# Attention on one core: nine slots per pair of sequences instead of ten, with the token transposes of the next pair inside the last projection

## The chip, the core and the metric

One core of a Trainium2 chip runs the whole program. The metric is the device time of one execution in microseconds (us), the median over runs. TensorE (PE) does matmuls and transposes, VectorE (DVE) and ScalarE (ACT) work from PSUM and SBUF, GpSimd (POOL) works from SBUF alone, and SyncE (SP) issues all the transfers.

## What is computed

```python
h = s4d_kernel(...)                       # 16 sequences x 128 channels x 1024
h = concatenate([h, txt], axis=1)         # 16 x 205 tokens x 1024
# attention, 32 heads of 32, ONE shared key and value head, causal, ALiBi
qkv = layernorm(h) @ Wqkv                 # 1024 x (1024 + 32 + 32)
p = softmax(causal(q k^T * 32**-0.5 + slope * (pos_k - pos_q)))
h = h + (p v) @ Wo
# feed forward: base linear, and a routed rank-16 LoRA of 8 experts
h = h + ffn(layernorm(h))
```

All of it is float32. Products that need full precision are made of three matmuls: each operand is split into a rounded `hi` part and the rest `lo`, and hi*hi, hi*lo and lo*hi are summed in one PSUM bank.

## The kernel before, in words

Three blocks follow one another: the mixer (the S4D kernel, into `h_dram`), attention, and the block with the output projection and the feed forward. The change lies in `attention_block` alone.

Attention goes by **pairs** of sequences: 8 pairs (`PAIRS`) of 410 tokens (`PT`). `visit` (L504) runs `body` once for pair 0, then a hardware loop (`Fori`) over pairs 1 to 6, once for pair 7, and once more (pair 8, `last is None`) to drain. So the loop branches back five times.

A pair has 10 **slots** (`SLOTS`), a slot has 8 **groups** (`GH`). In each group every engine does its piece of up to four strands. PE's order in a group is: the scores of one head, the three transposes of one head's probabilities (`turn`), a piece of the slot's main work, and in group 6 `values`.

- **Main work** (`MAIN`, L473): slot 0 is `"ln"`, the transposes of the normalised tokens `ht` into `xT` (one token tile and one half of the model dimension in each of the 8 groups); the other nine slots are projections (`("q", k)` or `"kv"`) of 8 x 3 matmuls of 410 columns each (`three`, L642).
- **Attention units**: a pair has 8 units j of 8 heads each. `SCORE_SLOT` gives the slot in which unit j's scores are made: 5, 6, 7, 8, 9, and 11, 12, 13, which are slots 1, 2 and 3 of the next pair. The probabilities of a unit are transposed in groups 4 to 7 of the slot behind (`tj`) and in groups 0 to 3 of the second slot behind (`aj`), where `values` also stands. So slots 0 and 4 have no scores.
- **The split of a main result**: ACT copies the bank rounded (`hi_part`), DVE subtracts (`lo_part`) and so frees the bank. All main work goes round three PSUM banks (`BANKS`), with one count of uses for the pair (`BANK_USES` 18, `USE`, `KV_USE`, `VT_USE`; semaphores `proj_done`, `hi_written`, `bank_read`).
- **DVE** in a group: `bias_head` (adds the mask to the scores and takes the minimum), then a `lo_part` if one is due, then at times a step of the next pair's layer norm (`ln_stats` from turn 12 on, then `ln_rstd`, `ln_apply` from turn 36 on; a turn is 8 * slot + group), then `copy_turned`, which copies the transposed probabilities out of PSUM.
- **SP** stacks q for the scores: `stack_q` (L545) issues three transfers from `q_hi` and `q_lo` into `Qs` in the slot after q was made. The scores of units 2g and 2g + 1 wait for the stacks of q 2g and 2g + 1 (`q_stacked`). SP also loads the next pair's tokens `ht`, in slot 1.

The lines that set PE's waits around the change:

```python
def three(out, w, cols, i):                                   # a projection, group i
def main_step(p, slot, what, i):
    if what == "ln":                                          # slot 0
        wait_count(pe, bank_read, BANK_USES * p + i - BANKS + 1)
def bias_head(p, j, i):                                       # DVE, waits for scores_done
def lo_part(p, slot, i):                                      # DVE, waits for hi_written
```

Of the kernel before, what the change touches and what calls it, by code (L numbers as in the profile page):

```python
# [24 lines left out]
S = CH + TXT  # L25
# [16 lines left out]
SLOTS = 10  # L42
BANKS = 3
BANK_USES = 18
# [372 lines left out]
def attention_block(nc, ctx, io, W):  # L417
# [41 lines left out]
    proj_done, hi_written, bank_read = sem("proj_done"), sem("hi_written"), sem("bank_read")  # L459
# [13 lines left out]
    MAIN = ["ln", ("q", 0), ("q", 1), "kv", ("q", 2), ("q", 3), ("q", 4), ("q", 5), ("q", 6), ("q", 7)]  # L473
    USE = {0: 8, 1: 9, 2: 11, 3: 12, 4: 14, 5: 15, 6: 16, 7: 17}
    KV_USE, VT_USE = 10, 13
    V_SLOT = 6
    LN_HI_AFTER, LN_LO_AFTER = 1, 2
    SCORE_SLOT = [5, 6, 7, 8, 9, 11, 12, 13]

    def hi_count(use):  # L480
        return use + 1 if use < VT_USE else use
# [47 lines left out]
    with nc.Block() as block:  # L529
        @block.sync  # L530
        def _(sp):
# [6 lines left out]
            def stack_q(p, k):  # L538
                g, r = k // 2, k % 2

                wait_apart(sp, bank_read, BANK_USES * p + USE[k] + 1, const_loaded, 32)
# [16 lines left out]
            def body(p, first, last):  # L558
                for slot, main, sj, tj, aj in slots(p, first, last):
                    if last is None and slot == 1:  # L560
# [12 lines left out]
                    if slot == 1 and last is True:  # L573
                        for k in range(4):
                            sp.wait_ge(proj_done, BANK_USES * p + 4 + k + 1)
                            load_wo(k)
# [21 lines left out]
        def _(pe):  # L598
            def scores(p, j, i):
                g, b = j // 2, j % 2  # L600
                if i == 0:
                    for q in q_stacked:
                        pe.wait_ge(q, 16 * STACKS * (4 * p + g + 1))
                    if j == 0:
                        pe.wait_ge(bank_read, BANK_USES * p + KV_USE + 1)
# [19 lines left out]
            def values(p, j):  # L625
# [3 lines left out]
                if j == 0:  # L629
                    pe.wait_ge(bank_read, BANK_USES * p + VT_USE + 1)  # L630
# [14 lines left out]

            def main_step(p, slot, what, i):
                if what == "ln":
                    wait_count(pe, bank_read, BANK_USES * p + i - BANKS + 1)
                    s, half = i % 4, i // 4
                    if half == 0:  # L650
                        pe.wait_ge(xn_ready, 4 * p + s + 1)
                    n = TILES[s][2]
                    for q in range(4):
                        last = nc.tensor.transpose(pr[i % BANKS][:, 128 * q:128 * q + n],
                                                   ht[0:n, s, (4 * half + q) * 128:(4 * half + q + 1) * 128], ident[0:n, 0:n])
                    last.then_inc(proj_done, 1)
                    return
                use = KV_USE if what == "kv" else USE[what[1]]
                if i == 0:
                    if slot == V_SLOT:  # L660

                        wait_apart(pe, bank_read, BANK_USES * p + VT_USE - BANKS + 1, const_ready)
                        for c in range(2):
                            nc.tensor.transpose(pr[VT_USE % BANKS][:, 64 * c:64 * c + HD], vT[96:128, c * S:c * S + CH], ident[96:128, 96:128])
                            last = nc.tensor.transpose(pr[VT_USE % BANKS][0:TXT, 64 * c + HD:64 * c + 2 * HD],
                                                       vT[96:128, c * S + CH:(c + 1) * S], ident[96:128, 96:128])
                        last.then_inc(proj_done, 1)
# [636 lines left out]
```

## Time and profile before

| what | before |
|---|---|
| median of 3 runs | 1744.44 us |
| the runs | 1738.39, 1744.44, 1744.45 us |
| span of the profiled execution, first to last instruction | 1737.4 us |
| PE busy over the span | 1523.9 us, 88% |
| DVE, ACT, POOL busy | 1132.7, 739.4, 537.0 us |
| ACT's split of four token transposes (`xT_hi`, L712), mean | 514 ns |
| mean granted TensorE clock | 0.946 of full |
| attention's projections, first to last | 222.57 to 950.97 us |

The profiled execution is told by its span alone; no time of its own stands beside it. The median lies 7.0 us above that span. In the views of the trace a matmul's busy time overlaps the next one's, since matmuls are pipelined; what a matmul costs PE is the distance from its start to the start of the next. "[2.15 <-X]" behind a row is the idle time of that engine just before it, and what ended it; "issue" is time in which nothing that the profile shows was waited for. A row of the windows view gives the stretch (us from the span's start), its length, then busy time and number of instructions of PE, PEld (weight loads), DVE, ACT and POOL, the mean granted clock, the busy share of the DMA engines and GB/s.

### The profile page before, as it was taken

How to read it: one execution, taken by the hardware profiler on the slowest of the kernel's cores; microseconds unless marked ns; L12 is line 12 of the kernel's file. 1: busy time of each engine (PE TensorE's matmuls, PEld its weight loads, DVE VectorE, ACT ScalarE, POOL GpSimd, SP SyncE). 2: the span in 40 equal slices, each digit the busy share in tenths (PEclk: the TensorE clock that was granted, in tenths of full speed). 3: DMA queues.
4: the chain of work that ended last, by engine and by line, in shares of the span. 5: the costliest groups of instructions: out<-in, count | busy, mean ns of one | idle time of the engine just before them, and what ended most of it. 6: DMA issues, size and time to landing. Idle time of an engine off the chain costs nothing. (4 is left out here: it accounts for less than half of the span.)

```text
span 1737.4 us, 31406 instructions
## 1 busy us (share of the span) xinstructions
PE 1523.9 (88%) x9622; PEld 1296.2 (75%) x9622; DVE 1132.7 (65%) x4116; ACT 739.4 (43%) x2624; POOL 537.0 (31%) x314
## 2 busy tenths in 40 slices
PE   0355399989999999999998769999999999999998
PEld 0355388878878788888887558888888888888886
DVE  7999378879787877879878854344443444444343
ACT  3455157776877767767878631101001010010100
POOL 1787314443534343444545401010110101011010
PEclk9876689999999999999999689999999999999999
DMA  6134455444554445444555341212112121121201
GB/s 200 37 88 94 103 98 109 80 78 91 87 103 73 103 73 103 78 79 97 87 118 86 102 174 37 73 42 67 61 47 72 36 72 48 60 72 36 73 34 38
DMA packets 110527, 139.63 MB, mean 80 GB/s; under 512 B 13156, under 2 KB 96484, under 8 KB 110040
## 3 DMA queue, kind: packets, MB, share of 16 engines
q1 hardware_dynamic: 110408, 138.41, 34.8%
q14 instruction: 89, 0.73, 0.2%
q8 instruction: 30, 0.49, 0.1%
HBM read 62.82 MB, written 40.30 MB: 59 GB/s over the span
## 5 line engine op out<-in xcount | busy, mean ns | idle before, releaser
L700 ACT ACTIVATE P<-P,nmax 128x128 f32<-128x128 f32 (+1 forms) x1024 | 434.3, 426 | 90.3 <-DVE nmax L790 84.0
L764 POOL TENSOR_TENSOR P<-P,rden 128x512 f32<-128x512 f32 (+1 forms) x256 | 329.2, 1308 | 449.2 <-DVE rden L796 449.0
L790 DVE CUSTOM_DVE_ANT_0 P<-sc,mask 128x128 f32<-128x128 f32 (+1 forms) x1024 | 292.3, 323 | 98.4 <-PE sc L612 91.9
L1116 POOL TENSOR_TENSOR h<-h,base_b 128x1024 f32<-128x1024 f32 (+1 forms) x26 | 84.7, 3260 | 637.5 <-DVE xn L1143 637.5
L802 DVE COPY PTR<-pt 128x282 f32<-128x282 f32 x512 | 222.3, 435 | 32.1 <-PE pt L622 18.7
L642 PE MATMUL pr<-xT_hi,wq_hi 128*128 128x410 f32 x576 | 242.4, 421 | 0.0
L642 PE MATMUL pr<-xT_lo,wq_hi 128*128 128x410 f32 x576 | 203.6, 353 | 0.0
L642 PE MATMUL pr<-xT_hi,wq_lo 128*128 128x410 f32 x576 | 202.6, 352 | 0.0
L700 ACT ACTIVATION_READ_ACCUMULATOR P<-P,nmax 128x1 f32 (+1 forms) x1024 | 191.8, 187 | 0.0
L1086 ACT ACTIVATE x2T_hi<-x 128x512 fp32r<-128x512 f32 (+1 forms) x52 | 28.0, 590 | 366.8 <-PE x L1050 366.8
L1028 PE MATMUL wo<-wq_hi,aT_hi 128*128 128x512 f32 (+1 forms) x416 | 168.9, 406 | 12.4 <-DVE aT_lo L1147 7.5
L620 PE MATMUL pt<-ident,P 128*128 128x128 f32 x512 | 152.1, 297 | 27.4 <-DVE PTR L802 26.9
L411 PE MATMUL mix_ps<-Q,X 128*128 128x128 f32 x512 | 75.0, 320 | 112.9 <-DVE Q L393 112.9
L1028 PE MATMUL wo<-wq_lo,aT_hi 128*128 128x512 f32 (+1 forms) x416 | 166.7, 401 | 0.0
L1028 PE MATMUL wo<-wq_hi,aT_lo 128*128 128x512 f32 (+1 forms) x416 | 166.0, 399 | 0.0
L1028 PE MATMUL b<-w_lo,x2T_hi 128*128 128x512 f32 (+1 forms) x416 | 165.8, 398 | 0.0
L1028 PE MATMUL b<-w_hi,x2T_hi 128*128 128x512 f32 (+1 forms) x416 | 164.0, 394 | 0.0
L1028 PE MATMUL b<-w_hi,x2T_lo 128*128 128x512 f32 (+1 forms) x416 | 163.4, 393 | 0.0
L411 PEld LDWEIGHTS mix_ps<-Q,X 128*128 128x128 f32 x512 | 73.7, 235 | 114.0 <-issue 114.0
L611 PE MATMUL sc<-Ks,Qs 100*128 100x128 f32 x512 | 130.6, 255 | 20.5 <-DMA Qs<-q_lo 13.1
L612 PE MATMUL sc<-Ks,Qs 100*77 100x206 f32 x512 | 140.9, 275 | 0.0
L611 PEld LDWEIGHTS sc<-Ks,Qs 100*128 100x128 f32 x512 | 99.8, 195 | 47.6 <-issue 32.0
(180 smaller groups left out, 3185.9 us busy)
## 6 DMA issues: line engine op xcount, KB each, us to landing
Qs<-q_hi SPq DMA_DIRECT2D x128, 205.0 KB, 4.7
Qs<-q_lo SPq DMA_DIRECT2D x64, 205.0 KB, 5.5
att_dram<-att SPq DMA_DIRECT2D x64, 205.0 KB, 2.4
at<-att_dram SPq DMA_DIRECT2D x25, 512.0 KB, 4.7
h<-h_dram SPq DMA_DIRECT2D x25, 512.0 KB, 3.4
out<-h SPq DMA_DIRECT2D x25, 512.0 KB, 2.6
h_dram<-Y SPq DMA_DIRECT2D x64, 128.0 KB, 3.1
ht<-h_dram SPq DMA_DIRECT2D x16, 512.0 KB, 5.1
```

The costliest lines, as they stand in the source:

```text
L411: last = nc.tensor.matmul(out, x[:, step % 2, j].rearrange("p a c -> p (a c)"), Q[:, step % QRING, j, :], start=first, stop=not first)
L611: nc.tensor.matmul(bank[:, 0:CH], q[:, 0:CH], Ks[0:QR, g // 2, b, 0:CH], start=True, stop=True)
L612: nc.tensor.matmul(bank[0:TXT, CH:CH + S + 1], q[:, CH:S], Ks[0:QR, g // 2, b, :], start=True, stop=True).then_inc(scores_done, 1)
L620: nc.tensor.transpose(bank[:, 0:CH], src[:, 0:CH], ident[:])
L642: last = nc.tensor.matmul(out, w[a][:, i, cols], xT[x][:, i, :], start=(i == 0 and m == 0), stop=(i == KC - 1 and m == 2))
L700: last = nc.scalar.activation(P[rows, j % 2, i, cols], P[rows, j % 2, i, cols], ACT.Exp, scale=-1.0, bias=nmax[at], accum_out=den[at])
L764: lastp = nc.gpsimd.tensor_tensor(w, w, r, ALU.mult)
L790: lastv = v.tensor_tensor_reduce(P[0:n, j % 2, i, cols], sc[i % 2][0:n, cols], mask[0:n, m], 1.0, 3.0e38, ALU.add, ALU.min, nmax[0:n, j % ...
L802: v.tensor_copy(PTR[:, j % 2, i, :], pt[i % 2][:, 0:S + TXT]).then_inc(pT_copied, 1)
L1028: last = nc.tensor.matmul(bank[0:n, 0:cols.stop - cols.start], lhs[a][:, k, 0:n], w[b][:, k, cols], start=(start and k == 0 and m == 0), s ...
L1086: nc.scalar.activation(xT[0][:, 4 * half:4 * half + 4, 0:n], src, ACT.Copy).then_inc(xT_hi, 1)
L1116: nc.gpsimd.tensor_tensor(h2[0:n, par, :], h2[0:n, par, :], base_b[0:n, :], ALU.add).then_inc(biased, 1)
```

## The change

- The slot `"ln"` goes; a pair has nine slots, in the order q0, q1, q2, kv, q3, ..., q7. q2 now stands ahead of kv.
- `SCORE_SLOT` becomes 5 to 12: units 0 to 3 in slots 5 to 8, units 4 to 7 in slots 0 to 3 of the next pair. Only slot 4 has no scores.
- The token transposes are grouped by chunk of the model dimension: `turn_ln(p, i)` makes chunk i for all four token tiles (four transposes into one bank). The next pair's stand in slot 8, behind the q7 matmuls of group i. They use banks 0 and 1 in turn; q7 has bank 2.
- ACT splits chunk i one group later (`hi_ln`), DVE two groups later and behind `bias_head` (`lo_ln`); chunks 6 and 7 fall into groups 0 and 1 of the next slot 0, for ACT chunk 7 alone. There q0's first group waits for the split of chunk 6.
- Pair 0's transposes are made ahead of the first slot, and the first waits until all four tiles are normalised.
- SP loads the next pair's tokens at the start of slot 0 instead of slot 1, ahead of the stack of q7.
- The bank counts are split into `main_*`, `ln_*` and `vt_*`.

```diff
-SLOTS = 10
+SLOTS = 9
...
-    MAIN = ["ln", ("q", 0), ("q", 1), "kv", ("q", 2), ("q", 3), ("q", 4), ("q", 5), ("q", 6), ("q", 7)]
+    MAIN = [("q", 0), ("q", 1), ("q", 2), "kv", ("q", 3), ("q", 4), ("q", 5), ("q", 6), ("q", 7)]
...
+    MAIN_BANK = [0, 1, 0, 1, 0, 1, 0, 1, 2]
+    VT_BANK = 2
     V_SLOT = 6
+    LN_SLOT = SLOTS - 1
     LN_HI_AFTER, LN_LO_AFTER = 1, 2
-    SCORE_SLOT = [5, 6, 7, 8, 9, 11, 12, 13]
+    SCORE_SLOT = [5, 6, 7, 8, 9, 10, 11, 12]
...
+                    if slot == 0 and last is False:
+                        sp.wait_ge(ln_turned, KC * p + KC)
+                        for s in range(4):
+                            load_h(p + 1, s)
...
-                    if slot == 1 and last is False:
-                        for s in range(4):
-                            sp.wait_ge(proj_done, BANK_USES * p + 4 + s + 1)
-                            load_h(p + 1, s)
...
+            def turn_ln(p, i):
+
+                if i == 0:
+                    pe.wait_ge(xn_ready, 4 * p + 4)
+                    wait_count(pe, main_read, SLOTS * p - 2)
+                elif i == 1:
+                    wait_count(pe, main_read, SLOTS * p - 1)
+                else:
+                    pe.wait_ge(ln_read, KC * p + i - 1)
+                for s, (c, t0, n) in enumerate(TILES):
+                    at = c * S + t0
+                    last = nc.tensor.transpose(pr[i % 2][:, at:at + n], ht[0:n, s, i * 128:(i + 1) * 128], ident[0:n, 0:n])
+                last.then_inc(ln_turned, 1)
...
+                    if slot == 0:
+                        pe.wait_ge(ln_read, KC * p + KC - 1)
+                    elif slot == 1:
+                        pe.wait_ge(ln_read, KC * p + KC)
+                    elif slot == SLOTS - 1:
+                        pe.wait_ge(vt_read, p + 1)
+                    else:
+                        pe.wait_ge(main_read, SLOTS * p + slot - 1)
+                if i == KC - 1 and slot == 0:
+                    pe.wait_ge(ln_read, KC * p + KC)
...
                         if main is not None:
                             main_step(p, slot, main, i)
+                        if slot == LN_SLOT and last is False:
+                            turn_ln(p + 1, i)
                         if i == 6 and aj is not None:
                             values(*aj)
             pe.wait_ge(const_ready, 1)
+            for i in range(KC):
+                turn_ln(0, i)
...
+            def hi_ln(p, i):
+                act.wait_ge(ln_turned, KC * p + i + 1)
+                nc.scalar.activation(xT[0][:, i, :], pr[i % 2][:, 0:PT], ACT.Copy).then_inc(ln_hi, 1)
...
+            def lo_ln(p, i):
+                dve.wait_ge(ln_hi, KC * p + i + 1)
+                v.tensor_tensor(xT[1][:, i, :], pr[i % 2][:, 0:PT], xT[0][:, i, :].bitcast(F32), ALU.subtract).then_inc(ln_read, 1)
...
                         if sj is not None:
                             bias_head(*sj, i)
+                        ln_at = GH * slot + i - LN_LO_AFTER
+                        if not first and last is not None and 0 <= ln_at + GH - KC + LN_LO_AFTER < LN_LO_AFTER:
+                            lo_ln(p, ln_at + GH)
...
+                        if slot == LN_SLOT and i >= LN_LO_AFTER and last is False:
+                            lo_ln(p + 1, i - LN_LO_AFTER)
```

How the instructions stand, at the places of which the prediction speaks. First PE in the loop of before, at the start of slot 0: `pt` is a transpose of probabilities, `pr<-ident,ht` the token transposes, and no projection matmul is among them.

```order
L620 MATMUL pt<-ident,P 128x128
L621 MATMUL pt<-ident,P 128x77
L622 MATMUL pt<-ident,P 77x77
L59 ISA
L651 ISA
L654 MATMUL pr<-ident,ht 128x128 x4
```

And PE in the changed kernel, one group of slot 8: `sc` are the scores, `pr<-xT` the three matmuls of q7.

```order
L614 MATMUL sc<-Ks,Qs 128x128
L615 MATMUL sc<-Ks,Qs 77x206
L623 MATMUL pt<-ident,P 128x128
L624 MATMUL pt<-ident,P 128x77
L625 MATMUL pt<-ident,P 77x77
L645 MATMUL pr<-xT_hi,wq_hi 128x410
L645 MATMUL pr<-xT_lo,wq_hi 128x410
L645 MATMUL pr<-xT_hi,wq_lo 128x410
L657 REGISTER_ALU
L660 MATMUL pr<-ident,ht 128x128
L660 MATMUL pr<-ident,ht 128x77
L660 MATMUL pr<-ident,ht 128x128
```

The four token transposes have moved from a slot without scores and projections to the end of a group that has both, behind a wait for `ln_read` (L657).

DVE in one group of the same slot 8: two pieces of `bias_head` (each with the read of its minimum), the `lo` part of the chunk turned two groups before, and the copy of the turned probabilities.

```order
L66 REGISTER_ALU
L808 ISA P,nmax<-sc,mask 128x128
L808 ISA nmax 128x1
L808 ISA P,nmax<-sc,mask 77x205
L808 ISA nmax 77x1
L823 REGISTER_ALU
L824 TENSOR_TENSOR xT_lo<-pr,xT_hi 128x410
L820 COPY PTR<-pt 128x282
```

Before, DVE had the token splits between copies alone, with no `bias_head` in slot 0:

```order
L812 TENSOR_TENSOR xT_lo<-pr,xT_hi 128x4x77
L799 REGISTER_ALU
L802 COPY PTR<-pt 128x282
L809 REGISTER_ALU
L812 TENSOR_TENSOR xT_lo<-pr,xT_hi 128x4x128
```

The `lo` part now stands behind a `bias_head` that waits for the same group's scores.

At the loop's end DVE branches straight into slot 0 with its `bias_head`, and the `lo` part of chunk 6 behind that:

```order
L820 COPY PTR<-pt 128x282
L511 REGISTER_ALU
L511 COMPARE_AND_BRANCH
L808 ISA P,nmax<-sc,mask 128x128
L808 ISA nmax 128x1
L808 ISA P,nmax<-sc,mask 77x205
L808 ISA nmax 77x1
L824 TENSOR_TENSOR xT_lo<-pr,xT_hi 128x410
```

Before, a copy of turned probabilities was the first thing behind the branch; now the first projection of the next pair hangs on the fifth row.

## Rows read from the trace of the kernel before

**Rows 1.** Windows by stretch, pair 3: slots 1, 2, 3-5, 6-7, 9, next 0.
```profile
490.82:499.09 8.27, 8.27 (x68) 7.13 (x67) 7.68 (x41) 6.33 (x27) 1.29 (x2) 1.00 0.79 214
499.09:508.65 9.56, 8.82 (x57) 7.01 (x56) 9.56 (x47) 8.48 (x38) 6.39 (x5) 1.00 0.57 102
508.65:535.99 27.34, 26.89 (x217) 22.82 (x215) 23.85 (x112) 18.33 (x73) 10.24 (x8) 1.00 0.37 62
535.99:556.79 20.80, 18.64 (x136) 17.24 (x136) 14.79 (x84) 15.68 (x68) 10.20 (x8) 0.92 0.46 71
566.60:575.70 9.10, 9.10 (x78) 8.10 (x77) 7.52 (x43) 7.72 (x32) 5.12 (x4) 1.00 0.56 92
575.70:587.05 11.35, 8.54 (x78) 7.39 (x77) 7.28 (x19) 5.10 (x13) 2.56 (x2) 0.85 0.46 78
```

**Rows 2.** Timeline, PE: start us, busy us. Slot 7, the wait for stacked q.
```profile
545.29 0.32 PE L611 MATMUL sc<-Ks,Qs 100*128 100x128 f32 x1 [2.15 <-DMA Qs<-q_lo]
```

**Rows 3.** Windows: the stretch behind that wait, pair 3 and pair 5.
```profile
546.30:549.70 3.40, 3.40 (x17) 3.35 (x16) 2.63 (x15) 1.94 (x9) 0.00 (x0) 0.50 0.03 10
739.10:742.50 3.40, 3.40 (x30) 3.40 (x30) 2.89 (x16) 1.89 (x8) 0.00 (x0) 1.00 0.00 0
```

**Rows 4.** Groups by line, DVE; timeline, PE, behind the branch at 576 us.
```profile
L802 DVE COPY PTR<-pt 128x282 f32<-128x282 f32 x512 | 222.3, 435 | 32.1 <-PE pt L622 18.7 <-issue 12.5
...
579.37 0.33 PE L620 MATMUL pt<-ident,P 128*128 128x128 f32 x1 [2.30 <-DVE PTR L802]
```

**Rows 5.** Timeline, PE: a full group of slot 8, from scores to next scores.
```profile
557.44 0.23 PE L611 MATMUL sc<-Ks,Qs 100*128 100x128 f32 x1
...
558.46 0.23 PE L611 MATMUL sc<-Ks,Qs 100*128 100x128 f32 x1
```

**Rows 6.** Timeline, DVE: the same group, `bias_head` and the instruction behind it.
```profile
557.91 0.29 DVE L790 CUSTOM_DVE_ANT_0 P<-sc,mask 128x128 f32<-128x128 f32 x1
...
558.42 0.57 DVE L823 SCALAR_TENSOR_TENSOR q_lo<-pr,q_hi 128x410 fp32r<-128x410 f32 x1
```

**Rows 7.** Timelines, DVE then PE: a `lo` part and the transposes it releases.
```profile
483.13 0.58 DVE L823 SCALAR_TENSOR_TENSOR q_lo<-pr,q_hi 128x410 fp32r<-128x410 f32 x1 [0.60 <-ACT q_hi L726]
...
483.85 0.32 PE L654 MATMUL pr<-ident,ht 128*128 128x128 f32 x1 [0.79 <-DVE q_lo L823]
```

**Rows 8.** Timeline, PE: four token transposes, and the next instruction.
```profile
479.60 0.60 PE L654 MATMUL pr<-ident,ht 128*128 128x128 f32 x4
480.04 0.27 PE L620 MATMUL pt<-ident,P 128*128 128x128 f32 x1
```

**Rows 9.** Timeline, DVE: layer-norm statistics between heads, slot 2.
```profile
507.24 0.68 DVE L840 BATCH_NORM_STATS2 stats<-ht 77x6 f32<-77x512 f32 x1
507.84 0.43 DVE L802 COPY PTR<-pt 128x282 f32<-128x282 f32 x1
508.19 0.28 DVE L790 CUSTOM_DVE_ANT_0 P<-sc,mask 128x128 f32<-128x128 f32 x1
```

**Rows 10.** Windows: pair 0, pairs 1-6, pair 7, each from first projection to next.
```profile
222.57:297.27 74.70, 71.46 (x513) 65.40 (x511) 56.05 (x253) 47.50 (x185) 25.55 (x20) 0.96 0.56 98
297.27:871.44 574.17, 539.48 (x4204) 467.73 (x4202) 471.56 (x2299) 420.82 (x1699) 245.45 (x192) 0.96 0.49 89
871.44:950.97 79.53, 77.49 (x626) 69.56 (x625) 62.91 (x340) 64.40 (x272) 38.32 (x30) 1.00 0.53 102
```

**Rows 11.** Windows: pair 0's slot 2, and its slot 9 with the next slot 0.
```profile
228.45:232.97 4.52, 4.52 (x26) 4.50 (x26) 3.58 (x9) 0.52 (x1) 0.00 (x0) 1.00 0.26 71
280.07:297.27 17.20, 16.65 (x156) 14.19 (x154) 14.59 (x59) 12.66 (x45) 7.68 (x6) 1.00 0.59 99
```

**Rows 12.** Timelines, DVE then PE: pair 0's tokens are normalised, then turned.
```profile
215.38 0.81 DVE L856 TENSOR_SCALAR ht<-ht,mv,rstd 128x1024 f32<-128x1024 f32 x1
...
216.34 0.87 PE L654 MATMUL pr<-ident,ht 128*128 128x128 f32 x3 [28.41 <-DVE ht L856]
```

**Rows 13.** Groups by line, DVE: the split of Wo, mostly in the drain.
```profile
L876 DVE TENSOR_TENSOR wq_lo<-ht,wq_hi 128x1024 fp32r<-128x1024 f32 x9 | 14.4, 1604 | 3.9 <-ACT wq_hi L743 3.9
```

More of the change, by code:

```diff
@@ L559, in body @@
                 for slot, main, sj, tj, aj in slots(p, first, last):
+                    if slot == 0 and last is False:
+                        sp.wait_ge(ln_turned, KC * p + KC)
+                        for s in range(4):
+                            load_h(p + 1, s)
+                    if slot == 0 and last is True:
+                        sp.wait_ge(ln_turned, KC * p + KC)
+                        for k in range(4):
+                            load_wo(k)
                     if last is None and slot == 1:
@@ new lines, in turn_v @@
+            def turn_v(p):
+                wait_apart(pe, main_read, SLOTS * p, const_ready)
+                for c in range(2):
+                    nc.tensor.transpose(pr[VT_BANK][:, 64 * c:64 * c + HD], vT[96:128, c * S:c * S + CH], ident[96:128, 96:128])
+                    last = nc.tensor.transpose(pr[VT_BANK][0:TXT, 64 * c + HD:64 * c + 2 * HD],
+                                               vT[96:128, c * S + CH:(c + 1) * S], ident[96:128, 96:128])
+                last.then_inc(vt_turned, 1)
@@ L672, in main_step @@
+                if i == KC - 1 and slot == 0:
+                    pe.wait_ge(ln_read, KC * p + KC)
+                out = pr[MAIN_BANK[slot]][:, 0:PT]
                 if what == "kv":
-                    last = three(pr[use % BANKS][:, 0:PT], wkv, slice(0, 128), i)
+                    last = three(out, wkv, slice(0, 128), i)
                 else:
-                    last = three(pr[use % BANKS][:, 0:PT], wq, slice(128 * what[1], 128 * what[1] + 128), i)
+                    last = three(out, wq, slice(128 * what[1], 128 * what[1] + 128), i)
@@ L749, in _ @@
             act.wait_ge(const_ready, 1)
+            for i in range(KC):
+                hi_ln(0, i)
             visit(body)(act)
@@ L816, in lo_part @@
+            def lo_part(p, slot):
+                what, src = MAIN[slot], pr[MAIN_BANK[slot]]
+                dve.wait_ge(main_hi, SLOTS * p + slot + 1)
+                if what == "kv":
+                    rows = src[HD:2 * HD, 0:PT].rearrange("p (b t) -> p b t", b=2)
                     for var in range(2):
                         at = Ks[HD:2 * HD, var, :, 0:S]
[L818 to L819 removed]
+                        lastv = v.tensor_tensor(at, rows, at.bitcast(F32), ALU.subtract)
+                    lastv.then_inc(main_read, 1)
@@ L909, in _ @@
                 ln_apply(0, s, link)
+            for i in range(KC):
+                lo_ln(0, i)
             visit(body)(dve)
```

111 lines of the change are left out of this document (31 added, 80 removed).

## The prediction

> **What bounds the kernel now.** I read the page first: PE is busy for 88% of the span and PE closes the chain that ended last. Then I cut one pair of attention into its slots with the windows view [rows 1]. In most slots PE is busy all the time. In slot 2 DVE is: 9.56 of 9.56 us, while PE has 8.82. The next pair's slot 0, which the change takes out, lasts 11.35 us with PE at a mean clock of 0.85. Slots 6 and 7 show 0.92.
>
> Two waits of PE explain these clocks. In slot 7 the scores of unit 2 wait 2.15 us for the stack of q3 [rows 2]. Right behind that wait the clock stands at 0.50, its 1.2 GHz level, for 3.4 us; in pair 5 the same wait leaves it at 1.00 [rows 3]. I take the fall as happening for five of the eight pairs (0 to 4) and its price as half of 3.4 us, 1.7 us. The other wait is the loop's branch. Behind it DVE stands still for five gaps of "issue", 12.5 us together, so 2.5 us each, and PE waits 2.30 us for DVE's copy [rows 4].
>
> **Unit prices.** A full group (scores, three transposes, three projection matmuls) takes PE 558.46 - 557.44 = 1.02 us [rows 5]. Slot 9 is eight of them and `values`: 9.10 - 8 x 1.02 = 0.94 for `values`. Slot 1 has four heads' transposes less: (9.10 - 8.27) / 4 = 0.21 a head [rows 1]. DVE begins `bias_head` 557.91 - 557.44 = 0.47 us after the scores begin, and its next instruction 0.51 us later [rows 5, 6]. A `lo` part lasts 0.58 us, and the transposes that wait for it begin 0.14 us after its end [rows 7]. Four transposes of 128 rows take 0.44 us [rows 8]; two of 128 and two of 77 rows are, in proportion, 0.35.
>
> **The change slot by slot, for a pass of the loop.**
>
> - *Slot 8* holds slot 9's old work and the token transposes. Their own time is 8 x 0.35 = 2.8 us. But from group 1 on they wait for a `lo` part that DVE does behind the same group's `bias_head`: 0.47 + 0.51 + 0.58 + 0.14 = 1.70 us after the scores began, and PE arrives at 1.02. That is 0.68 us of waiting in 7 groups, 4.8 us. A chain in such an order can't be hidden by work behind it, since PE's queue is in order. ACT has the room: its work in a slot is at most 8.48 us [rows 1], and eight copies of 0.51 are added. The period of a group is 1.70 + 0.35 = 2.05 us. Slot 8: 9.10 + 2.8 + 4.8 = 16.7 us.
> - *Slot 0* has the scores of unit 4, so again slot 9's work, 9.10 us. At its head stands the branch. Counted from the last group's scores, DVE ends its copy (0.43 [rows 9]) at 0.47 + 0.51 + 0.58 + 0.43 = 1.99 us, stands still for 2.5, does `bias_head` (0.51) and chunk 6 (0.58), and PE goes on 0.14 later, at 5.72. PE itself arrives at 2.05 plus scores and transposes, 1.02 - 4.52 / 8 = 0.46 (a bare projection slot is 4.52 us [rows 11]): 2.5. The wait is 3.2 us, longer than the 2.30 of now. I take the clock to fall behind it as in slot 7, 1.7 us. Slot 0: 14.0 us.
> - *Slot 1* gains four heads' transposes, 9.10 us for PE. From group 4 on DVE also has statistics: 0.51 + 0.60 + 0.35 = 1.46 us a group [rows 6, 9], 0.44 over PE's 1.02 in three groups, of which `values` gives 0.94 back. Slot 1: 9.5 us.
> - *Slot 2* is DVE's already. It gains four copies of 0.35: 9.56 + 1.4 = 11.0 us; PE's four transposes and `values` are hidden behind that.
> - *Slots 3 to 5* keep what they have: 27.34 us [rows 1].
> - *Slots 6 and 7* lose the wait for q3. q3 is made in slot 4 and stacked in slot 5, two slots ahead of its scores, where now it is stacked in the slot just ahead. 20.80 - 2.15 - 1.7 = 16.95 us.
>
> Sum: 14.0 + 9.5 + 11.0 + 27.34 + 16.95 + 16.7 = 95.5 us a pass. The loop's six pairs now take 574.17 / 6 = 95.7 us [rows 10]. So dropping a slot of 11.35 us gives back nearly all of it: its work isn't gone but rides in slots 1 and 2, where DVE is short, and in slot 8, where it forms a chain.
>
> **SP's queue.** The four loads of tokens now stand ahead of the stack of q7. That stack waits for DVE's `lo` part of q7 in group 1 of slot 0 anyway, and its scores come in slot 2, over 20 us later; the loads are 1.6 MB. I cost it at nothing. If that cover were gone, the wait of 2.15 us would come back there (a rival below). The statistics of the loaded tokens begin in slot 1, group 4, as before.
>
> **The whole.** The branch back occurs five times, for pairs 2 to 6: 5 x 95.5 = 477.5. Pair 1 is entered without it: the wait is 0.47 + 0.51 + 0.58 + 0.14 from slot 0's first scores, against 0.46, so 1.25 us, and no fall of the clock: 95.5 - 1.7 - 1.95 = 91.85. Pair 0: from 74.70 go the wait and its clock (3.85), the old slot 0 (17.20 - 9.10 = 8.1 [rows 11]) and unit 4 (9.10 - 4.52 = 4.6), and slot 8 brings 7.6: 65.75. Pair 7: 79.53 - 2.15 + 1.25 + 0.83 + 0.83 + 0.94 = 81.2. Together 716.3, against 74.70 + 574.17 + 79.53 = 728.4 [rows 10]: **12.1 us less**.
>
> Ahead of that, pair 0's transposes waited for one normalised tile, 216.34, and will wait for four of some 0.75 us from 215.38 on, until 218.5 [rows 12]. Then two banks go round: transposes at half clock 0.6, ACT's copy 0.51, `lo` 0.58, three hand-offs of 0.14, so 2.1 us for two chunks; q0 needs the seventh, 3 x 2.1 + 2.0 = 8.3 us. q0 begins at 226.8 instead of 222.57: 4.2 us more. Behind it, the drain's slot 0 gets unit 4's scores beside four splits of Wo of 1.6 us on DVE [rows 13], which bounds there: 8 x 0.51 = 4.1 us more. The sum is -12.1 + 4.2 + 4.1 = **-3.8 us**. It is made against the span of 1737.4; the median lies 7.0 above, and I carry the difference over: 1744.4 - 3.8 = **1741 us**. A measurement of this kernel tells about 0.5%, 8.7 us, from no change, so this is no change.
>
> **Bounds.** The wait in slot 8 is the largest unknown, since no row shows that chain as a whole. At least it is nothing (33 us less in 7 slots), if DVE somehow kept ahead; at most DVE also lags by a copy, 0.35 more a group (17 us more). I take 0.68, where the parts lie in rows. The fall of the clock in slot 0 lies between none (8.5 us less) and twice 3.4 us (8.5 more).
>
> **Rivals.**
>
> - *Faster: cheaper hand-offs.* A `lo` part may be followed 0.08 before its end, as the copy of 0.43 is [rows 9], and PE's 0.14 may overlap weight loading; with DVE's 0.47 a little shorter the wait is 0.45, which is 0.23 x 49 = 11 us less. If the clock also stays up behind the branch, as it did in pair 5 [rows 3], 8.5 more go: 1741 - 20 = 1721 us. For it: single rows are bounds, not means. Against: the branch's wait is longer than the one of rows 2.
> - *Much faster: no chain in slot 8.* 1741 - 33 = 1708 us. The order on DVE speaks against it.
> - *Slower: the clock falls inside slot 8.* PE would pause 0.68 us in every 2.05, a third of the time. The rows know pauses of 0.3 in 1.5 us in slot 2, at a clock of 1.00, and 2.15 us, which brought 0.50 [rows 1 to 3]; this lies between. At half clock a group of PE's own work is 2 x 1.37 = 2.7 us instead of 2.05. If half of slot 8 goes so, it costs 8 x 0.7 / 2 + 0.5 = 3.3 us, seven times: 1741 + 23 = 1764 us. It decides from 3.8 + 8.7 = 12.5 us on, so if three of the eight groups run at 0.50. The Trainium skill (TensorE: Matmul & The Clock Gate, "A second HAM failure mode: psum-queue depth-cycling") describes such a case: PE pausing briefly between groups of matmuls, because it cycles through PSUM banks, often enough to make the clock go back and forth. By that rule the change would be slower, at this rival's time. Slot 2's row speaks against it, for smaller pauses.
> - *Slower: the wait for stacked q only moves*, behind the token loads, to slot 2. 1741 + 8 x 2.15 + 5 x 1.7 = 1767 us.
>
> **How the numbers follow.** The forecast has 0.43, cheaper hand-offs 0.27, no chain 0.05, the clock in slot 8 0.19, the moved wait 0.06. The forecast's own spread reaches over both marks of 0.5%, more on the faster side, which is nearer. So faster 0.35, same 0.40, slower 0.25. The range goes from 1716, a little beyond the first rival, to 1765, which holds the third.
>
> **What would show it.** Right: slot 8 of some 16 to 17 us with PE's token transposes waiting for DVE's xT_lo some 0.7 us, 49 times; a wait of about 3 us for xT_lo at the head of slot 0; no wait for Qs in slot 7; slot 2 at 11 us with DVE busy throughout; a pass of about 95 us. Wrong: a slot 8 near 12 us, a granted clock of 0.50 inside slot 8, slot 1 or 2 much longer than said, or a wait for Qs in slot 2.

## The result, and the profile after

| what | before | after |
|---|---|---|
| median, runs made together | 1743.7 us (10 runs) | 1750.2 us (10 runs, 1748.1 to 1752.7) |
| ratio, 95% interval | | 1.0036 (1.0024 to 1.0047) |
| span of the profiled execution | 1737.4 us | 1748.4 us |
| attention's projections, first to last | 222.57 to 950.97 | 229.83 to 957.94 us |

The forecast was 1741, 3.8 us less. The kernel became 6.5 us slower. That is inside the 0.5% called no change, and inside the range. But the sign is wrong and the two differences lie 10 us apart, and with this many runs the interval excludes no change at all.

The two spans differ by 11.0 us, in three places. Attention begins 7.3 us later. Its passes take 728.11 instead of 728.40 us. What follows takes 4.0 us more. First the windows view of the changed kernel by pairs, which answers to [rows 10]:

```profile
229.83:296.51 66.68, 62.92 (x414) 57.45 (x414) 45.41 (x206) 39.78 (x154) 17.87 (x14) 0.97 0.55 92
296.51:877.26 580.75, 534.82 (x4200) 461.87 (x4200) 471.34 (x2299) 421.60 (x1699) 245.53 (x192) 0.98 0.50 88
877.26:957.94 80.68, 80.68 (x663) 72.25 (x664) 65.03 (x345) 64.42 (x268) 40.91 (x32) 1.00 0.57 106
```

Pairs 0 and 7 are near the forecast (65.75 and 81.2). The loop's six pairs are not: 580.75 against 477.5 + 91.85 = 569.35. So I cut one pass, pair 3, in the same view. The rows are slot 0 from its first projection, slots 1, 2, 3 to 5, 6 and 7, and slot 8 up to the first projection of the next pass:

```profile
490.28:501.18 10.90, 10.90 (x80) 9.90 (x81) 7.74 (x40) 6.61 (x28) 5.12 (x4) 0.86 0.91 199
501.18:510.64 9.46, 9.46 (x83) 8.50 (x82) 9.19 (x47) 8.26 (x35) 5.12 (x4) 1.00 0.09 30
510.64:521.81 11.17, 10.30 (x83) 8.67 (x82) 11.17 (x53) 8.29 (x35) 5.12 (x4) 1.00 0.90 132
521.81:548.87 27.06, 26.70 (x216) 22.75 (x214) 23.54 (x109) 17.98 (x73) 10.24 (x8) 1.00 0.41 70
548.87:565.69 16.82, 16.82 (x137) 15.78 (x136) 14.53 (x84) 15.46 (x68) 10.20 (x8) 1.00 0.62 88
565.69:587.20 21.51, 14.62 (x115) 11.03 (x114) 12.35 (x56) 13.69 (x50) 5.12 (x4) 0.96 0.30 55
```

The forecast for these rows was 10.8 (14.0 less the wait at the head, which lies in the last row here), 9.5, 11.0, 27.34, 16.95 and 19.9 (16.7 and the wait of 3.2). Five of six hold within 0.3 us. The last is 1.6 too long. Slot 0 is not always so short: in the five passes behind a branch it takes 11.97, 10.90, 11.88, 12.38 and 11.05 us.

The waits view of the changed kernel names who keeps PE waiting in attention:

```profile
PE pr L645 <- DVE xT_lo L824: 21.0, 8, 3.7
PE pr L660 <- DVE xT_lo L824: 19.2, 45, 0.6
PE pr L660 <- DVE q_lo L837: 2.9, 7, 0.4
```

Of the second row's 45 waits three stand ahead of attention, and 42 are the chain in slot 8: groups 2 to 7, seven times, 0.43 us each in the mean. In group 1 the same wait is ended by the `lo` part of q6, the row below it. The view begins the wait where the modelled end of the last projection matmul lies, so it shows less than the 0.7 us that the period costs. The first row holds the wait at the head of slot 0, 3.7 us at the branches. A row for scores that wait for `Qs` is no longer there. PE's timeline shows two groups inside slot 8, 2.08 us apart, then the slot's last group and the head of slot 0:

```profile
568.75 0.31 PE L614 MATMUL sc<-Ks,Qs 100*128 100x128 f32 x1
...
570.83 0.31 PE L614 MATMUL sc<-Ks,Qs 100*128 100x128 f32 x1
...
580.36 0.33 PE L614 MATMUL sc<-Ks,Qs 100*128 100x128 f32 x1
...
582.08 0.58 PE L660 MATMUL pr<-ident,ht 128*128 128x128 f32 x4 [0.43 <-DVE xT_lo L824]
582.77 0.32 PE L614 MATMUL sc<-Ks,Qs 100*128 100x128 f32 x1
...
587.20 0.71 PE L645 MATMUL pr<-xT_hi,wq_hi 128*128 128x410 f32 x1 [3.75 <-DVE xT_lo L824]
```

And DVE's, over the same stretch:

```profile
581.45 0.57 DVE L824 TENSOR_TENSOR xT_lo<-pr,xT_hi 128x410 fp32r<-128x410 f32 x1
581.95 0.44 DVE L820 COPY PTR<-pt 128x282 f32<-128x282 f32 x1
586.06 0.29 DVE L808 CUSTOM_DVE_ANT_0 P<-sc,mask 128x128 f32<-128x128 f32 x1 [3.68 <-issue]
```

PE takes 2.41 us from scores to scores across the branch, nearly its pace of 2.08 in the slot. DVE ends its copy at 582.39 and starts again at 586.06. The standstill is 3.68 us, and 3.72, 3.64, 3.66 and 3.69 at the other four branches. It was taken as 2.5.

What followed it is in the windows view again: the stretches at half clock behind the branches of 391 and 490 us.

```profile
391.10:397.90 6.80, 5.53 (x23) 5.44 (x24) 4.35 (x19) 3.03 (x13) 1.02 (x2) 0.50 0.99 273
490.10:493.50 3.40, 3.22 (x13) 3.16 (x14) 1.86 (x8) 1.36 (x8) 0.00 (x0) 0.51 1.05 314
```

Of the five branches three have 6.8 us at 0.50 and two have 3.4. But the kernel before has the same three and two. Its stretches behind the branches of 385 and 674 us:

```profile
385.90:392.70 6.80, 6.53 (x39) 5.99 (x43) 6.05 (x14) 3.10 (x7) 2.56 (x2) 0.50 0.66 94
676.00:682.80 6.80, 6.44 (x40) 5.63 (x44) 5.69 (x14) 2.48 (x6) 2.55 (x2) 0.50 0.66 94
```

The forecast took the length of 3.4 us from the wait in slot 7, and not from these rows.

Ahead of attention, the timelines of DVE and of PE, against [rows 12]:

```profile
218.00 2.98 DVE L870 TENSOR_SCALAR ht<-ht,mv,rstd 128x1024 f32<-128x1024 f32 x4
```

```profile
221.13 1.60 PE L660 MATMUL pr<-ident,ht 128*128 128x128 f32 x8 [33.33 <-DVE ht L870]
223.32 1.63 PE L660 MATMUL pr<-ident,ht 128*128 128x128 f32 x8 [0.60 <-DVE xT_lo L824]
```

The mixer let the normalising begin at 218.00 instead of 215.38. From there q0 takes 229.83 - 218.00 = 11.8 us, before 222.57 - 215.38 = 7.2 us: 4.6 us are the change's. The other 2.6 us are scatter of the mixer, which the change doesn't touch: over the other profiled kernels of this study the normalising begins between 214.2 and 218.2 us, with old and new order alike.

### The profile page after: what moved, and what is told of

It reads as the page before. It is cut to its first block and busy times, and to the rows that moved or that the text cites. A ratio compares the mean times of both kernels' runs of the same rounds, so it can differ in the third digit from the quotient of the medians.

```text
span 1748.4 us, 31354 instructions
## 1 busy us (share of the span) xinstructions
PE 1520.3 (87%) x9622; PEld 1286.9 (74%) x9622; DVE 1130.6 (65%) x4116; ACT 740.9 (42%) x2624; POOL 536.6 (31%) x314
## 5 line engine op out<-in xcount | busy, mean ns | idle before, releaser
L645 PE MATMUL pr<-xT_hi,wq_hi 128*128 128x410 f32 x576 | 247.0, 429 | 21.0 <-DVE xT_lo L824 21.0
L623 PE MATMUL pt<-ident,P 128*128 128x128 f32 x512 | 148.6, 290 | 16.9 <-DVE PTR L820 15.5
L645 PEld LDWEIGHTS pr<-xT_hi,wq_hi 128*128 128x128 f32 x576 | 111.9, 194 | 22.8 <-DVE xT_lo L824 22.4
```

Source lines behind the costliest of these rows:

```text
L623: nc.tensor.transpose(bank[:, 0:CH], src[:, 0:CH], ident[:])
L645: last = nc.tensor.matmul(out, w[a][:, i, cols], xT[x][:, i, :], start=(i == 0 and m == 0), stop=(i == KC - 1 and m == 2))
```

## The experiments

Each ratio is to the kernel before, run beside it, with its 95% interval. The pass given with a kernel is pair 3, from q0 to the next q0 (96.23 before, 96.92 after). Differences in us are between medians. The kernel before had 1741.0 us beside the first four runs told here, those of the chain in slot 8 and of the written-out loop, and 1743.4 to 1744.0 beside the others. So a difference between kernels of different rounds is uncertain by some 3 us, and where the ratios tell less than the medians, both are given. Two questions: where do the 10 us between forecast and result lie, and what is the chain in slot 8 worth?

### The chain in slot 8

```diff
+                        if slot == LN_SLOT and i >= LN_LO_AFTER and last is False:
+                            lo_ln(p + 1, i - LN_LO_AFTER)
                         if sj is not None:
                             bias_head(*sj, i)
...
-                        if slot == LN_SLOT and i >= LN_LO_AFTER and last is False:
-                            lo_ln(p + 1, i - LN_LO_AFTER)
```

> The changed kernel, but in slot 8 DVE does the lo part of chunk i-2 ahead of the group's bias_head instead of behind it. Theory (the chain scores, bias_head, lo part, token transposes sets slot 8): the group's period falls from 2.07 us to about 1.4, slot 8 loses some 0.68 x 7 = 4.8 us, seven times: 33 us off the changed kernel, about 1717 us. Rival (slot 8 is simply full, DVE and ACT can't do more in it): under 10 us off, and the period stays near 2.

Measured: 1728.6 us, ratio 0.992 (0.990 to 0.994), 21.6 us less than the changed kernel, where 33 were expected. So the chain is real and is a matter of order on DVE. Part of what slot 8 gained came back as a longer wait at the head of slot 0, where chunk 6 still stands behind `bias_head`. PE's row there:

```profile
574.43 0.71 PE L645 MATMUL pr<-xT_hi,wq_hi 128*128 128x410 f32 x1 [4.74 <-DVE xT_lo L824]
```

That is 4.7 us at the branches, where the changed kernel has 3.7. In slot 8 PE's scores now follow each other like this:

```profile
560.64 0.31 PE L614 MATMUL sc<-Ks,Qs 100*128 100x128 f32 x1
562.08 0.31 PE L614 MATMUL sc<-Ks,Qs 100*128 100x128 f32 x1
563.50 0.31 PE L614 MATMUL sc<-Ks,Qs 100*128 100x128 f32 x1
```

The period is 1.43 us, not 2.08 as in the changed kernel and not PE's own 1.37. DVE's work in a group is 0.51 for `bias_head` [rows 6], 0.50 and 0.44 by the rows of the changed kernel above, 1.45 us, so DVE is what bounds slot 8 once the chain is gone. The same edit, made in slot 0 as well:

```diff
                         ln_at = GH * slot + i - LN_LO_AFTER
                         if not first and last is not None and 0 <= ln_at + GH - KC + LN_LO_AFTER < LN_LO_AFTER:
                             lo_ln(p, ln_at + GH)
+                        if sj is not None:
+                            bias_head(*sj, i)
```

> The same, and in groups 0 and 1 of slot 0 too, so that the first instruction of DVE behind the loop's branch is the lo part of chunk 6 and not bias_head. Theory A (the branch costs DVE 3.7 us instead of 2.5 because of what bias_head needs computed behind it): the gap goes back to about 2.5 us, the wait of PE at the head of slot 0 falls by 0.5 + 1.2 us in five passes, 8 us less than the first variant and more if the half clock shrinks. Rival B (the gap depends on the loop's body, not on its first instruction): the gap stays at 3.7, 0.5 us in seven places, 3.5 us less.

Measured: 1721.1 us, ratio 0.988 (0.986 to 0.990), 7.5 us less than the run before it. That is near the 8 us of theory A, but its cause falls: the standstill did not shorten, though another instruction now stands first behind the branch. In both kernels DVE ended its last copy 0.5 us sooner after slot 8's last scores, and still started again at the same distance from them, 5.6 to 5.7 us. Its standstill is 4.04 to 4.08 us in the second kernel and 4.14 to 4.20 in the first:

```profile
573.29 0.29 DVE L808 CUSTOM_DVE_ANT_0 P<-sc,mask 128x128 f32<-128x128 f32 x1 [4.18 <-issue]
```

So the standstill isn't a fixed cost counted from DVE's branch. In these two kernels something that goes by the scores ends it.

### The branch

The hardware loop is written out, in the changed kernel and in the one before:

```diff
-            with eng.Fori(1, PAIRS - 1) as p:
+            for p in range(1, PAIRS - 1):
                 body(p, False, False)
```

> The changed kernel with the hardware loop over pairs 1 to 6 written out, so without branches back. Theory (the branch and the half clock behind it cost 3.7 - 1.0 us of waiting, 0.3 us on PE and 2.6 us of half clock): 5 x 5.6 = 28 us less, and 1.00 as granted clock from slot 0 on. Rival (the wait at the head of slot 0 is the lo part's chain, the branch only overlaps it): under 10 us.

Measured: 1719.0 us, ratio 0.986 (0.984 to 0.988).

> The kernel before with its loop written out. Theory: it loses PE's wait of 2.1 us and 1.7 to 2.5 us of half clock five times, 19 to 23 us less than before. Together with the unrolled changed kernel it shows how much of the difference between the two kernels is the branch: 7 us or so. Rival: both gain the same and the difference stays.

Measured: 1722.0 us, ratio 0.988 (0.986 to 0.990). Written out, the changed kernel is 3.0 us faster than the one before. With the loop it is 6.5 us slower. By the medians the branches, with the clock behind them, cost 22 us before and 31 us after; in the traces attention shrinks by 19 and 30 us. By either count the change made the branches 9 to 11 us dearer, which is nearly the whole miss.

### What prolongs the standstill

SP's timeline of the changed kernel at that branch:

```profile
580.82 1.19 SPq L548 DMA_DIRECT2D Qs<-q_hi  x2
582.07 0.61 SPq L548 DMA_DIRECT2D Qs<-q_lo  x1
582.94 0.38 SPq L555 DMA_DIRECT2D att_dram<-att  x1
584.00 2.00 SPq L539 DMA_DIRECT2D ht<-h_dram  x4
```

And of the kernel before, in its slot 9:

```profile
568.95 1.20 SPq L545 DMA_DIRECT2D Qs<-q_hi  x2
570.20 0.61 SPq L545 DMA_DIRECT2D Qs<-q_lo  x1
575.49 0.38 SPq L552 DMA_DIRECT2D att_dram<-att  x1
```

The stack of q6 went out 2.4 us into slot 9, 7 us ahead of DVE's last instruction before the branch. It has to wait until unit 3 has read that half of `Qs` (`wait_count(sp, scores_done, 64 * p + 16 * g - 16)`). Unit 3's scores stand in slot 8 in both kernels. Before, the stack of q6 stood a slot later, so the wait was over. Now it stands in slot 8 itself, and goes out with the slot's last scores, 0.46 us after 580.36. First I moved every transfer but one small store away from the branch:

```diff
+                    if slot == 0 and not first:
+                        stack_q(p - 1, 7)
+                        stack_q(p - 1, 6)
                     if slot == 0 and last is False:
                         sp.wait_ge(ln_turned, KC * p + KC)
...
-                    if main is not None and slot >= 1 and isinstance(MAIN[slot - 1], tuple):
+                    if main is not None and 1 <= slot < SLOTS - 1 and isinstance(MAIN[slot - 1], tuple):
                         stack_q(p, MAIN[slot - 1][1])
-                    if slot == 0 and not first:
-                        stack_q(p - 1, 7)
```

> The changed kernel, but SP stacks q6 no longer in slot 8, just ahead of the loop's branch, but in slot 0 behind the stack of q7, which waits for DVE's lo part of q7, and loads the tokens behind both. So no transfer but one small store is in flight while the engines branch. Theory F (code behind the branch comes through the DMA engines and queues behind the stack of q6 and the token loads): DVE's gap falls from 3.7 us to about 2.5, the projection of slot 0 begins 1.2 us earlier in each of five passes, 6 us less, and up to 4 more from shorter half clocks. Rival P (the gap comes from the longer program of the loop or from bias_head standing first): the gap stays at 3.7 and the time within 2 us of the changed kernel's.

Measured: 1768.0 us, ratio 1.013 (1.012 to 1.015), 17.8 us more than the changed kernel instead of less. The standstill did fall, to 2.29 to 2.40 us, and the last stretch of the pass to 20.2. But slot 1 grew from 9.46 to between 11.4 and 16.0 us. Its waits view and ACT's timeline name the new wait:

```profile
ACT q_hi L742 <- DMA Qs<-q_lo: 21.1, 7, 4.3
```

```profile
511.14 0.51 ACT L742 ACTIVATE q_hi<-pr 128x410 fp32r<-128x410 f32 x1 [2.46 <-DMA Qs<-q_lo]
```

`q_hi` has one place for even and one for odd q. The next pair's q0 can't be rounded before q6 has been stacked, and PE's bank isn't free before that. That was my edit's fault, and the run says nothing of the price of the standstill. The same edit in a version with the lo parts first in slots 8 and 0, and with the statistics of the next tokens 20 turns later (`STATS_AT` 32 for 12, `APPLY_AT` 56 for 36, every second turn), where slot 2 is DVE's:

> The changed kernel, still looped, with lo parts first, transfers away from the branch, and the next pair's layer-norm statistics moved from slots 1 to 3 into slots 4 to 6 and the normalising into slot 7. Theory (slot 2 is DVE's): slot 2 falls from 11.1 to about 9.5 us and slot 3 from 9.8 to 9.4, 2 us in six pairs, 12 us, on top of 29 us for lo first and 6 for the branch: about 1703 us. Rival: the statistics only move the bound to slots 5 to 7: 1712 us or more.

Measured: 1755.5 us, ratio 1.007 (1.005 to 1.009). The wait of `q_hi` is there as well, and 1703 us were expected. The later statistics are a loss too. Slots 2 to 7 of pair 3 in this kernel,

```profile
515.67:573.68 58.01, 54.65 (x432) 46.98 (x430) 52.26 (x247) 42.26 (x175) 26.47 (x20) 1.00 0.54 84
```

and in the next but one of the kernels below, which has the lo parts first and the statistics where they were:

```profile
497.71:552.69 54.98, 53.71 (x432) 47.12 (x430) 49.19 (x244) 41.70 (x175) 25.58 (x20) 1.00 0.57 88
```

Slot 2 falls from 11.14 to 9.46 us, but slots 5 to 7 grow by 0.9, 1.3 and 2.3 us. Next, one transfer at a time. The token loads alone go back behind the stack of q7:

```diff
-                    if slot == 0 and last is False:
-                        sp.wait_ge(ln_turned, KC * p + KC)
-                        for s in range(4):
-                            load_h(p + 1, s)
...
                     if slot == 0 and not first:
                         stack_q(p - 1, 7)
+                    if slot == 0 and last is False:
+                        sp.wait_ge(ln_turned, KC * p + KC)
+                        for s in range(4):
+                            load_h(p + 1, s)
```

> The changed kernel, with one edit on SP alone: in slot 0 the four token loads stand behind the stack of q7 again, not ahead of it. The stacks of q6 and q7 stay where the change has them, so the wait of ACT's q_hi for a stack, which made the kernel with both stacks moved 18 us slower, can't arise. Theory A (DVE's standstill behind the branch is prolonged by the token loads that run across it): the gap of DVE falls from 3.7 to about 2.4 us at five branches, slot 8 with the wait at slot 0's head from 21.5 to 20.2 us, so 5 x 1.3 = 6.5 us less: about 1744 us, and more if the clock's fall in slot 0 gets shorter. Theory B (the stack of q6, issued in slot 8, is what prolongs it): gap and time as in the changed kernel, 3.7 and 1750 us. Theory C (loads that come some us later make the statistics of slot 1 late): a longer slot 1 than 9.46 us, and over 1750 us.

Measured: 1749.2 us, ratio 1.0037 (1.0025 to 1.0049), and a standstill of 3.66 to 3.70 us. Theory A, with the token loads as the cause, falls. The same edit in the version with the lo parts first:

> The changed kernel with the hardware loop kept, the lo parts of the token chunks ahead of bias_head in slots 8 and 0, and the token loads behind the stack of q7. Without the last edit it took 1721.1 us. Theory A (the loads prolong DVE's gap): 5 x 1.3 us less, 1714 to 1715 us. Theory B (they don't): 1721 us.

Measured: 1720.1 us, ratio 0.986 (0.984 to 0.988). That is 1.0 us from the kernel without that edit, so theory B holds here too. Then the stack of q6 alone, behind DVE's restart, early enough for q0:

```diff
-                    if main is not None and slot >= 1 and isinstance(MAIN[slot - 1], tuple):
+                    if main is not None and 1 <= slot < SLOTS - 1 and isinstance(MAIN[slot - 1], tuple):
...
+                    if slot == 0 and not first:
+                        wait_count(sp, scores_biased, 64 * (p - 1) + 33)
+                        stack_q(p - 1, 6)
```

> The changed kernel, with one edit on SP alone: the stack of q6 is issued in slot 0, once DVE has biased the first head there, that is once DVE has restarted behind the branch, instead of at the end of slot 8, where the changed kernel's wait for the scores of unit 3 lets it go just ahead of the branch (issued 580.82, DVE's code packets of 8 KB at about 583 take 0.9 to 1.0 us each, against 0.31 to 0.37 where the engines' queue is quiet). Unlike the kernel in which it stood behind the stack of q7, it lands long before slot 1, so ACT's q_hi has nothing to wait for. Theory A (q6's packets hold up the code DVE fetches at the branch): DVE's gap 2.3 to 2.4 instead of 3.7 us, slot 8 with the wait at slot 0's head 20.2 instead of 21.5, slot 1 as before at 9.46: 5 x 1.3 = 6.5 us less than 1750, about 1743. Theory B (the gap was shorter there since SP's whole order, or the late loads, had shifted): gap 3.7 and 1750 us. Either way, if the clock's longer fall in slot 0 hangs on the longer pause, some of the 6.8 us stretches at half clock become 3.4 and up to 4 us more go.

Measured: 1739.1 us, ratio 0.998 (0.997 to 0.999), 11.1 us less than the changed kernel by the medians and 9.8 by the ratios. Theory A expected 6.5, and up to 4 more from the clock. The standstills at the first three branches, DVE's timeline:

```profile
387.31 0.29 DVE L811 CUSTOM_DVE_ANT_0 P<-sc,mask 128x128 f32<-128x128 f32 x1 [2.47 <-issue]
...
482.94 0.29 DVE L811 CUSTOM_DVE_ANT_0 P<-sc,mask 128x128 f32<-128x128 f32 x1 [2.33 <-issue]
...
578.48 0.29 DVE L811 CUSTOM_DVE_ANT_0 P<-sc,mask 128x128 f32<-128x128 f32 x1 [2.24 <-issue]
```

Its slot 0, and its slot 8 up to the next first projection, in pair 3:

```profile
484.10:495.15 11.05, 11.05 (x81) 10.03 (x81) 7.87 (x40) 6.82 (x30) 5.12 (x4) 0.85 0.99 197
559.55:579.62 20.07, 14.60 (x115) 11.04 (x113) 12.36 (x56) 13.36 (x48) 5.12 (x4) 1.00 0.07 23
```

These were forecast as 10.8 and 19.9. Slot 0 is 11.05 or 11.06 us at all five branches, and nowhere is the clock at 0.50 for more than 3.4 us. The pass is 95.5 us, as forecast. The edit gave the pause 5 x 1.4 = 7 us and slot 0, now 11.05 instead of 11.64 in the mean, another 3. Those 3 us are the clock's, and it isn't shown that they hang on the pause. In the run with the transfers moved away from the branch the standstill was as short, 2.29 to 2.40 us, and four of five branches had 6.8 us at 0.50.

What the standstill coincides with is the windows view over it, in the changed kernel, with the token loads later, with the stack of q6 later, and in the kernel before (there, the second to last column is the DMA engines' share):

```profile
582.39:586.06 3.67, 0.95 (x9) 0.61 (x7) 0.00 (x0) 0.95 (x4) 0.00 (x0) 0.94 1.09 141
```

```profile
581.34:585.01 3.67, 0.95 (x9) 0.61 (x6) 0.00 (x1) 0.95 (x4) 0.00 (x0) 1.00 1.10 141
```

```profile
576.24:578.48 2.24, 0.96 (x9) 0.62 (x7) 0.01 (x1) 0.13 (x2) 0.00 (x0) 1.00 0.20 62
```

```profile
576.11:578.86 2.75, 0.95 (x12) 0.80 (x9) 0.00 (x1) 0.62 (x4) 0.00 (x0) 1.00 0.25 82
```

DVE stands still for 3.67 us where the stack of q6 fills the DMA engines, and for 2.24 to 2.75 where they are at least three quarters idle. The transfers view over the same stretches lists, by queue, packets, MB and their time as a share of 16 engines. The changed kernel:

```profile
q1 hardware_dynamic: 357, 0.50, 106.7%
q14 instruction: 2, 0.02, 2.6%
```

And the one with the stack of q6 later:

```profile
q1 hardware_dynamic: 165, 0.12, 18.6%
q14 instruction: 2, 0.02, 1.9%
```

Two packets of the instruction queue came in each stretch. They took 0.026 x 16 x 3.67 / 2 = 0.76 us each beside the stack's packets, and 0.019 x 16 x 2.24 / 2 = 0.34 us without. That the stack prolongs the standstill is shown by moving it. How it does so stays open. My reading is that DVE waits for its code behind the stack's packets, and it fits the restart at a fixed distance from the scores, since they release the stack. But no run isolates it, and these packets account for part of the time at most: the same view over 583.10 to 586.06 us has none of them. So with 0.76 us each they had landed by about 583.9, and DVE began 2.2 us later. With the stack later none starts behind 577.10, and DVE began at 578.48.

> The changed kernel with the loop kept, the lo parts of the token chunks ahead of bias_head in slots 8 and 0 (1721.1 us so far, with DVE restarting 5.6 us after the last group's scores although it had ended 0.5 us sooner), and the stack of q6 issued after DVE's restart. Theory A: the restart is no longer pinned by q6's packets, so slot 8 with the wait falls from 17.6 to 16.0 us at five branches: 1721 - 8 = 1713 us. Theory B: 1721 us.

Measured: 1708.7 us, ratio 0.981 (0.979 to 0.984); pass 90.7. That is 12.4 us less than without the edit by the medians, 11 by the ratios, where 8 were expected. The pause before q0 is 2.4 to 2.7 us instead of 4.1, five times 1.6. The rest is mostly slot 0, over the five passes 53.7 us against 57.9 in the loop version before this one; one pass has 9.50, without a fall of the clock.

### What nine slots are worth

PE waits for the odd stack only where head 4 reads it, in the kernel **before**:

```diff
-                if i == 0:
-                    for q in q_stacked:
-                        pe.wait_ge(q, 16 * STACKS * (4 * p + g + 1))
+                if i % 4 == 0:
+                    pe.wait_ge(q_stacked[i // 4], 16 * STACKS * (4 * p + g + 1))
+                if i == 0:
```

> The kernel before, but PE waits for the stack of the odd q only at head 4 of a unit, where it is first read, and not at head 0. It measures the wait for stacked q by itself, which the change removed by its order. Theory: PE no longer waits in slot 7 (2.15 us, eight times) and its clock stays up (1.7 us, four or five times), 24 us less than before. Rival (the wait is only moved to head 4 or to DVE): under 8 us less.

Measured: 1712.7 us, ratio 0.981 (0.978 to 0.984), 31 us less than the kernel before, where 24 were expected; pass 93.4. Slots 6 and 7 of that pass are 7.37 + 9.45 = 16.82 us, where before they were 20.80 [rows 1], the same as in the changed kernel. So the gain that the new order of the projections brings to slots 6 and 7 was to be had by one wait, without a slot less. Then both with the loop written out, first nine slots (lo parts first in slots 8 and 0), then ten (wait split):

> The changed kernel with lo parts first in slots 8 and 0, and with the loop written out. Theory (chain and branch are separate costs and add): 29 us for the first and 31 for the second, less what both count of the wait at the head of slot 0, so 50 to 57 us off the changed kernel, 1693 to 1700 us. Rival (each only uncovers the other): 1705 us or more.

Measured: 1686.1 us, ratio 0.967 (0.965 to 0.969), below the 1693 to 1700 expected; its pass in the windows view:

```profile
462.40:549.40 87.00, 85.62 (x703) 75.72 (x701) 77.92 (x384) 69.61 (x285) 40.94 (x32) 1.00 0.56 98
```

> The kernel before (ten slots), with PE's wait for the odd stack only at head 4, and the loop written out. It shows what nine slots are worth when both kernels are without the wait for stacked q and without the branch: the nine-slot one, with its lo parts first, took 1686.1 us. From the kernel before with the split wait (1712.7) and what the branch cost it (1744.0 - 1722.0 = 22 us): about 1691 us, so that nine slots are worth some 5 us. Rival: the two edits take the same clock time away twice, and it stays at 1697 us or more; second rival: below 1686 us, and nine slots are worth nothing even without their chain.

Measured: 1692.5 us, ratio 0.970 (0.968 to 0.972):

```profile
475.00:563.40 88.40, 86.60 (x704) 75.59 (x702) 78.49 (x384) 69.73 (x285) 40.91 (x32) 1.00 0.52 96
```

| | ten slots | nine slots |
|---|---|---|
| as given, with the loop | 1743.7 | 1750.2 |
| no wait for `Qs`, standstill below 2.8 us | 1712.7 | 1739.1 |
| and the lo parts first (nine slots only) | | 1708.7 |
| no branch, otherwise as the row above | 1692.5 | 1686.1 |

Nine slots with the chain are 26 us slower than ten, once both are free of the wait for stacked q. Without the chain they are 6 us faster with the loop written out, 1684.7 to 1686.5 against 1691.3 to 1693.7 us. With the loop the medians are 4 us apart, but the runs overlap and both ratios are 0.981, so there no difference is shown. The version at 1686.1 us beats both given kernels, by 3.3% and 3.7%.

## Why the prediction was wrong

- **Slot 8's chain: right.** 2.08 us a group against 2.05, with a wait for a `lo` part in 49 groups, 42 times for `xT_lo` and 7 times for q6's. The rivals with cheaper hand-offs and with no chain are out, and the edit that turned the order round shows that the order makes the chain.
- **Slots 1 to 7: right,** 64.5 us together against 64.8. Slot 2 is DVE's throughout (11.17 of 11.17), slots 6 and 7 lost the wait and the fall of the clock. PE nowhere waits for `Qs`, so the last rival is out.
- **The clock in slot 8: it didn't fall.** In the kernel with the late stack of q6 the row of slot 8 and the pause behind it shows 1.00 (559.55 us); the 0.96 in the changed kernel's row lies in the pause behind the slot. Pauses of 0.7 in 2.08 us left the clock up. The Trainium skill's rule of PE cycling through PSUM banks (TensorE: Matmul & The Clock Gate, "A second HAM failure mode: psum-queue depth-cycling") doesn't bite at this size of pause.
- **The head of slot 0: the step that failed,** and with it the paragraph on SP's queue. I wrote "stands still for 2.5", a number of the kernel before, and of the queue "I cost it at nothing". I looked at q7's stack and the token loads. The token loads don't matter: with them moved the time stayed. The step that I missed is q6's stack, which moved one slot forward onto the end of the slot whose scores release it, and so onto the branch. The standstill became 3.7 us, and the row that holds it is 1.6 us too long, 8 us over five passes. With that stack moved the standstill is 2.2 to 2.5 us, and the kernel 10 to 11 us faster. It then takes 1739.1 us against the forecast of 1741, and its attention 718.3 us against 716.3. So the other terms of the sum hold, with some luck: in this run the clock fell for the forecast's 3.4 us at each branch, which it doesn't in the kernel before.
- **The clock behind the branch: taken too low.** Slot 0 was forecast with one fall of 3.4 us, 10.8 us from its first projection, and has 11.64 in the mean, 4 us over five passes. The fall of 3.4 us was read off the wait in slot 7. Behind the branches of the kernel before stood 6.8 us three times in five already, which I didn't look up. The bounds of the forecast allow for it ("twice 3.4 us"), the sum doesn't.
- **The wait at the head** was 3.2 by my sum and 2.3 to 2.5 in PE's rows of the kernel with the late stack of q6, since the view counts it from a modelled end; the stretch as a whole, 20.1 against 19.9, is what bears comparison.
- **Ahead and behind: right.** 4.6 against 4.2 us until q0, 4.0 against 4.1 in the drain. The profiled span has 2.6 us more from the mixer's scatter, which the medians don't show: they lie 6.5 us apart where the spans lie 11.0.

## What to carry to other kernels

When a step moves, list every transfer that moves with it, and for each the semaphore that releases it: it can't go out before the release, wherever it stands in the queue. A hardware loop's branch is a spot of its own; what runs there is paid for several times, by the engine's standstill and by the clock behind it. Read the price of each pause from its own rows: the fall of the clock behind the branch was not that in slot 7. And before a slot is taken out, try the one wait that the slot's order causes: here that alone gave 31 us.

## What was not expected of the hardware

The standstill behind a branch differs by engine and is no constant. In the changed kernel PE goes on after 2.41 to 2.47 us from scores to scores, with hardly a gap. ACT has 2.71 to 2.76 us in the changed kernel and 2.17 to 2.21 with the stack of q6 later. DVE has 3.64 to 3.72 and 2.24 to 2.47 us. DVE's standstill even grew, to 4.2 us, when its work ended earlier. How long the clock stays at 0.50 behind a branch doesn't follow PE's pause alone. Behind pauses of about 3.7 us it was 6.8 us in three of five branches of the changed kernel. Behind pauses of 1.9 to 2.3 us it was 6.8 in three of five in the kernel before, and behind 2.3 to 2.5 us in four of five with the stacks and the token loads moved, but in none with the stack of q6 alone moved. In the last loop version, with pauses of 2.4 to 2.7 us, one branch in five had no fall at all. What decides between these is open.
